# Router logits computed in token order, with the activations as the stationary operand

## The reference

```python
shared_out = _expert(x, shared_gate, shared_up, shared_down)
routing_probs = jax.nn.sigmoid(x @ router_w + routing_bias)   # (tokens, 3)
scores, indices = jax.lax.top_k(routing_probs, 2)
scores = scores / scores.sum(axis=-1, keepdims=True)
combine_w = (one_hot(indices, 3) * scores[..., None]).sum(axis=-2)
...                                # three routed experts, each silu(x@g)*(x@u)@d
combined = jnp.einsum('ebsh,bse->bsh', out_e, combine_w)
return shared_out + combined
```

## Time and profile before

| | us |
|---|---|
| median of three runs | 1599.58 (1598.1 to 1603.18) |
| profiled execution | 1602.77 |
| its span | 1601.0 |
| PE busy | 1579.0 (99%) |
| PE weight loads busy | 1483.5 (93%) |
| DVE busy | 1199.1 (75%) |
| ACT busy | 879.1 (55%) |
| POOL busy | 408.6 (26%) |
| PE clock granted, mean | 0.997 |

### The profile page before, as it was taken

One profiled execution on the slowest core, in us unless ns is written; L12 is line 12 of the kernel. 1 busy time (PEld: TensorE's weight loads), 2 busy tenths in 40 slices (PEclk: granted clock), 3 DMA queues, 4 the chain that ended last, 5 costly groups with the idle time before them and its releaser, 6 DMA issues.

```text
span 1601.0 us, 46493 instructions
## 1 busy us (share of the span) xinstructions
PE 1579.0 (99%) x16632; PEld 1483.5 (93%) x16632; DVE 1199.1 (75%) x3387; ACT 879.1 (55%) x1896; POOL 408.6 (26%) x647
## 2 busy tenths in 40 slices
PE   7999999999999999999999999999999999999999
PEld 7799999999999999999999999999999999998998
DVE  6777787777877777877777877777877777877765
ACT  4556555555555565555565555565555566555542
POOL 1232321223212323212323212323212323212320
PEclk9999999999999999999999999999999999999999
DMA  6311211112111111111111111111111111111000
GB/s 248 106 52 60 70 55 46 50 58 69 61 41 39 44 49 57 57 39 39 43 49 57 57 39 39 44 50 57 57 38 40 44 50 57 57 35 35 34 33 14
DMA packets 75382, 86.81 MB, mean 54 GB/s; under 512 B 12720, under 2 KB 64328, under 8 KB 75208
## 3 DMA queue, kind: packets, MB, share of 16 engines
q1 hardware_dynamic: 65192, 66.85, 12.2%
q10 hardware_dynamic: 10144, 19.34, 3.8%
HBM read 32.44 MB, written 12.51 MB: 28 GB/s over the span
## 4 chain that ended last, share of the span: by engine, by line
PE 91%; DMA 4%; DVE 3%; SPq 1%; issue 1%; ACT 0%; POOL 0%; DVEq 0%
PE ps L439 83%; PE ps L442 6%; DMA kt<-kt 3%; PE ps L646 2%; DVE kt L1233 1%; DMA h<-in_txt 1%; DVE o L1130 1%; SPq L373 0%; DVE rotated L1221 0%; DVE xt L1161 0%; DVE qk_split L1226 0%; DVE stats L1150 0%; DVE rotated L1193 0%; POOL rstd L1075 0%; DVE h L1254 0%
## 5 line engine op out<-in xcount | busy, mean ns | idle before, releaser
L439 PE MATMUL ps<-xt,wf 64*128 64x326 f32 x6912 | 595.9, 316 | 0.0
L439 PEld LDWEIGHTS ps<-xt,wf 64*128 64x128 f32 x6912 | 533.5, 186 | 10.9 <-ACT qt L840 5.5
L439 PE MATMUL ps<-w_down_s,ht 128*128 128x192 f32 (+1 forms) x2304 | 414.9, 329 | 0.0
L439 PEld LDWEIGHTS ps<-w_down_s,ht 128*128 128x128 f32 (+1 forms) x2304 | 350.9, 174 | 14.9 <-issue 0.2
L1107 DVE SCALAR_TENSOR_TENSOR gated<-tanh_g,ps 128x326 f32<-128x326 f32 x384 | 188.9, 492 | 132.7 <-ACT tanh_g L854 132.3
L865 ACT ACTIVATE probs<-ps 128x792 f32<-128x792 f32 (+1 forms) x384 | 254.5, 663 | 23.1 <-PE ps L439 23.1
L854 ACT ACTIVATE tanh_g<-ps 128x326 f32<-128x326 f32 x384 | 170.1, 443 | 169.0 <-PE ps L439 166.4
L1066 POOL TENSOR_TENSOR probs<-probs,causal 128x512 f32<-128x512 f32 x192 | 228.8, 1192 | 133.6 <-ACT probs L865 133.6
L847 ACT ACTIVATE rows<-h,rstd 128x192 f32<-128x192 f32 (+2 forms) x279 | 151.1, 564 | 194.7 <-POOL rstd L1077 192.3
L1060 POOL TENSOR_TENSOR probs<-probs,causal 69x140 f32<-69x140 f32 x192 | 89.1, 464 | 475.4 <-ACT probs L865 475.4
L1113 DVE TENSOR_TENSOR ht<-gated,ps 128x326 f32<-128x326 f32 x384 | 190.1, 495 | 13.1
(11 more groups left out here) (108 smaller groups left out, 2003.7 us busy)
## 6 DMA issues: line engine op xcount, KB each, us to landing
kt<-kt SPq DMA_DIRECT2D x384, 40.8 KB, 1.9
x_s<-in_xp ACTq DMA_DIRECT2D x36, 384.0 KB, 3.1
qt<-qt SPq DMA_DIRECT2D x130, 81.5 KB, 2.0
residual<-h SPq DMA_DIRECT2D x31, 288.0 KB, 2.4
out<-o SPq DMA_DIRECT2D x32, 192.0 KB
qt<-qt ACTq DMA_DIRECT2D x62, 81.5 KB, 2.0
kept_rows<-embed_rows SPq DMA_DIRECT2D x40, 96.0 KB, 1.7
h<-kept_rows SPq DMA_DIRECT2D x30, 95.2 KB
```

The lines of the kernel that those rows point to most:

```text
L439: return nc.tensor.matmul(dst, lhs, rhs, start=first, stop=last)
```

## The change

The router's operands trade places. For each of the three token tiles, six products take the tile's columns of `xt2` as the stationary operand and stream the 4 columns of `wr`: 18 products, whose results lie tokens on partitions. VectorE adds the bias (now a 128x4 tile, positive), 9 numbers per partition, into `route` (`route_logits`), at the end of its turn behind `keep_k`. ScalarE takes exp(-x) of these 9 numbers (`route_up`). `route_turn` with its three products, its bank, its signal and its two waits goes, and `route_sum` reads `route` in SBUF instead of PSUM, in place. Score piece 0 now waits for the bias addition instead of the exponential, and unit 2 takes over the wait for the third kt group from `route_turn`. A memset and a sign change of the opening go too.

```diff
+                for t in range(TILES):
+                    for j in range(BLOCKS):
+                        for x in range(2):
+                            last = mm(ps[0:TILE_COLS[t], ROUTER_BANK, t * R_COLS:(t + 1) * R_COLS],
+                                      xt2[:, j, x, tile_cols(t)], wr[:, j, :], j + x == 0, j + x == BLOCKS)
...
-            def route_turn(b, A):
-                pe.wait_ge(route_exp.sem, route_exp.at(b, 1))
-                if A:
-                    pe.wait_ge(kt_kept.sem, kt_kept.at(b + 1, GROUPS))
-                for t in range(TILES):
-                    last = mm(ps[:, ROUTE_BANK, t * P:t * P + R_COLS], route_e[0:H, t * P:(t + 1) * P], ident[0:H, 0:R_COLS],
-                              True, True)
...
+            def route_up(b):
+                act.wait_ge(route_seen.sem, route_seen.at(b, 1))
+                nc.scalar.activation(route[:, 1], route[:, 0], ACT.Exp, scale=-1.0).then_inc(route_exp.sem, 1)
...
+            def route_logits(b):
+                dve.wait_ge(router_done.sem, router_done.at(b, 1))
+                logits = shaped(ps[:], [[R_COLS, TILES], [1, EXPERTS]], ROUTER_BANK * 512)
+                v.tensor_tensor(route[:, 0], logits, shaped(router_bias[:], [[0, TILES], [1, EXPERTS]]),
+                                ALU.add).then_inc(route_seen.sem, 1)
...
-                dve.wait_ge(route_turned.sem, route_turned.at(b, 1))
-                e = shaped(ps[:], [[P, TILES], [1, EXPERTS]], ROUTE_BANK * 512)
-                v.tensor_scalar(route[:, 1], e, 1.0, None, ALU.add).then_inc(route_seen.sem, 1)
+                dve.wait_ge(route_exp.sem, route_exp.at(b, 1))
+                v.tensor_scalar(route[:, 1], route[:, 1], 1.0, None, ALU.add).then_inc(route_raised.sem, 1)
...
@@ turn of VectorE, behind keep_k(2, b1, KEEP_BANK)
+                    route_logits(b2)
```

More of the change, by code:

```diff
@@ L70 @@
 KEEP_BANK = [6, 7, 2, 3, 6, 7]
-XT_BANK, YT_BANK, EMBED_BANK, ROUTER_BANK, ROUTE_BANK, PROJ_BANK = 6, 4, 2, 0, 7, 0
+XT_BANK, YT_BANK, EMBED_BANK, ROUTER_BANK, PROJ_BANK = 6, 4, 2, 0, 0
 SPLIT_PARTS = len(SPLIT_AT) - 1
@@ L111, in build @@
         bias_rows = sb("bias_rows", [P, 2, DIM])
-        router_bias = sb("router_bias", [R_COLS, 1])
+        router_bias = sb("router_bias", [P, R_COLS])
         cos_t = sb("cos_t", [P, TILES, HEAD_DIM // 2])
@@ L211, in build @@
         router_done = signal("router_done", 1)
-        route_turned = signal("route_turned", 1)
         n1_applied = signal("n1_applied", 1)
@@ L249, in build @@
         route_seen = signal("route_seen", 1)
+        route_raised = signal("route_raised", 1)
         gate_used = signal("gate_used", UNITS)
@@ L508, in unit @@
                         pe.wait_ge(qt_kept.sem, qt_kept.at(b + 1, GROUPS))
-                    pe.wait_ge(route_seen.sem, route_seen.at(b, 1))
+                        pe.wait_ge(kt_kept.sem, kt_kept.at(b + 1, GROUPS))
                 else:
@@ L524, in score @@
                 elif F:
-                    pe.wait_ge(route_exp.sem, route_exp.at(b - 1, 1))
+                    pe.wait_ge(route_seen.sem, route_seen.at(b - 1, 1))
                 if n % 2 == 0:
@@ L699, in turn @@
                         unit(k, b3, at, D, A)
-                        if k == 0:
-                            route_turn(b3, A)
                     if A:
@@ L935, in turn @@
                 if A:
-                    act.wait_ge(router_done.sem, router_done.at(b2, 1))
-                    nc.scalar.activation(route_e[0:R_COLS, 0:COLS], ps[0:R_COLS, ROUTER_BANK, 0:COLS], ACT.Exp, scale=-1.0,
-                                         bias=router_bias[:, 0:1]).then_inc(route_exp.sem, 1)
+                    route_up(b2)
             def start_norm1(b):
@@ L1047, in _ @@
                 keep_high(j, xt2[:, j, 0, :], N2_BANK[j], n2_turned, 0, xt2_hi)
[L1048 to L1051, removed]
+            route_up(0)
             turns(act, turn)
@@ L1373, in turn @@
                     sum_up(6, b3, L)
+                    if A:
+                        route_logits(b2)
             def split_ffn(j):
@@ L1393, in _ @@
             v.memset(row_sum[:], 1.0)
-            v.memset(route_e[:], 0.0)
             dve.wait_ge(s_bias, 16)
@@ L1406, in _ @@
             dve.wait_ge(s_const, 16 * 6)
-            v.tensor_scalar(router_bias[:], router_bias[:], -1.0, None, ALU.mult)
             v.tensor_copy(ident_r[:], ident[:]).then_inc(s_halve, 1)
@@ L1462, in _ @@
             v.tensor_scalar(w_down_s[:], w_down_s[:], 0.5, None, ALU.mult).then_inc(s_halve, 1)
+            route_logits(0)
             turns(dve, turn)
@@ L1518 @@
         "w_route": w_route, "w_down": w_down,
-        "b_router": b_router.reshape(R_COLS, 1),
+        "b_router": np.tile(b_router, (P, 1)),
         "rot_cos": rot_cos, "rot_sin": rot_sin, "mask": mask,
```

8 lines of the change are left out of this document (1 added, 7 removed).

## The result

| | before | after |
|---|---|---|
| median of the runs, us | 1601.28 (4 runs, 1598.10 to 1603.18) | 1618.46 (4 runs, 1617.06 to 1624.39) |
| profiled execution, us | 1602.77 | 1624.39 |
| its span, us | 1601.0 | 1622.6 |
| PE clock granted, mean | 0.997 | 0.985 |

The changed kernel is slower: ratio 1.0105, 95% interval 1.0087 to 1.0124. I had predicted 1601.8, between 1596.5 and 1619.5, with "within 0.3%" as the likeliest case. The time lies in the range, at the number of rival 1 (1618.5), but the likeliest case did not happen, and rival 1's mechanism is only a small part of the loss, as will be seen. The prediction also named a wait on VectorE ahead of units 4 to 6 as a sign of being wrong; there are two such waits, 0.8 us in all.

The account below looks back on a forecast made before the run. TensorE, busy 99% of the span, was taken as the bound. Router +0.80 less route_turn 0.66 gave +0.14 us in 12 turns, less elsewhere: about +2.2 on 1599.6, so 1601.8 us, range 1596.5 to 1619.5.

Parts of the forecast that it names:

- within 0.3%: Whole kernel: a time within 4.8 us of before, not to be told from no change; chance of same 0.45.
- rival 1: VectorE's last small routing operation (L1283) stands behind GpSimd's large mask; unit 6 at 10.3, about +19 us, 1618.5; chance 0.27.
- a wait on VectorE ahead of units 4 to 6: Sign in TensorE's waits: a wait on DVE ahead of these units would make the prediction wrong.
- The router, 1.80 us and +0.80: TensorE, first router product to unit 0: 18 products paced by stationary loads take 1.80 us instead of 1.00.
- upper bound of 0.95: Router's added time per turn if all 18 loads go at 0.12 us without a discount.
- route_turn, 0.66 us: TensorE between unit 0 and score piece 0: without its six loads, unit 1 and everything behind come 0.66 earlier.
- The DMA of kt: Score piece 0 waits for the DMA in 19 of 31 turns; up to 0.14 us of that wait vanishes.
- VectorE ahead of unit 6: VectorE gets back 0.6 us from mask collisions; up(3) ends at 9.15, ahead of unit 6 at 9.27.
- the walk: VectorE's new turn: route_sum 3.08 to 3.40, last small operation at 4.25, large mask 4.20 to 5.39.
- The margin of 0.05 us: VectorE's L1283 at 4.25 against GpSimd's large mask at 4.20; the times rest on sums of ten terms.
- What costs nothing: VectorE at the turn's end: the last expert's sums still end near 1.33, ahead of unit 1 at about 1.6.

Follow-up runs that it names:

- second kernel: Changed kernel with router operand padded to 128 columns, plus the last expert's sums moved ahead of route_logits: 1632.38 us, 1.0174 of before.
- third: As the second kernel, with the routing chain moved from units 0 and 1 to units 6 to 10: 1602.60 us, 0.9988 of before.
- fifth kernel: As the second kernel, with route_sum alone moved ahead of VectorE's products of unit 0: 1604.04 us, 0.9999 of before.
- sixth kernel: As the third, with the router's moving operand narrow again, 4 columns instead of 128: 1617.90 us, 1.0091 of before.
- first kernel: Changed kernel with the router's moving operand padded with zeros from 4 to 128 columns: 1612.13 us, 1.0047 of before.
- fourth kernel: Kernel before the change, with 18 narrow products added behind its own router, results unused: 1659.66 us, 1.034 of before.

## Why the prediction was right or wrong

**The router, 1.80 us and +0.80:** right (1.78). The rate of loading by the earlier trace rows carried over to a place with other streams. The upper bound of 0.95 was summed wrongly: all 18 loads at 0.12 give 2.16, with the 0.10 until unit 0 that is 1.26 more than before; 0.95 needs the six loads of 70 columns to stay near 0.06.

**route_turn, 0.66 us:** right where nothing else held unit 1: the last product of unit 1 starts at 2.92 behind unit 0 in turns 0, 1 and 30 and at 2.93 in the second, third and fifth kernels, 3.60 before.

**The DMA of kt:** right in kind, too small in size. TensorE's wait for it fell from 3.5 us in 9 waits to 1.4 in 2; behind 440 us, in the looped turns, from 2.6 in 8 to none (its weight loads alone still show 1.7 in 7, of 3.8 in 11). Rows of the waits, before and after:

```profile
PE ps L439 <- DMA kt<-kt: 3.5, 9, 0.9
```

```profile
PE ps L438 <- DMA kt<-kt: 1.4, 2, 1.2
```

The prediction let at most 0.14 us of each wait vanish, and counted nothing for the turns with a longer one. In the sixth kernel, which has the same narrow router and neither late sums nor a collision, the last product of unit 1 starts at 2.92 to 3.20 in the turns at full clock; before it was 3.60 to 4.25. So of the up to 0.65 that this wait had added, 0.28 at most was left, and turns that had waited long became shorter.

**VectorE ahead of unit 6:** the walk held to some hundredths: route_sum from 3.08 to 3.40, L1277 at 4.25. The margin of 0.05 us was the right place to doubt, and its answer is plain: started behind the mask by 0.05 to 0.07 us (second kernel, turns 0, 1 and 30 here), the operation stands to the mask's end; 0.16 ahead of it (turn at 631.36) or 0.09 (turn 28), it passes. The first kernel has the closest case: in its turn 7 both start at 431.46, the operation 0.003 us ahead, and it passes in 0.16. The walk's own mask at 4.20 would have lost; I should have read L1277 at 4.25 against 4.20 as a collision, since in every row the one that started first kept the way, and given rival 1 the greater chance. Rival 1's own sum has a slip too: up(1) at 6.4 against unit 4 at 6.17 is a wait of 0.23 there and not 0.37, which is the difference at unit 6 (10.3 against 9.93). The Trainium skill (SBUF — State Buffer, "Who interferes with whom") says that the order of issue decides who blocks. The runs agree in both directions: the operation takes 0.15 us when it starts ahead of the mask and 1.16 when it starts behind.

**"What costs nothing" failed.** The prediction had the last expert's sums end near 1.33 as before and unit 1 unharmed. They end at 1.76, since VectorE now comes to the loop's branch only behind route_logits, which waits for the router, and is then idle; the trace has the idle time in VectorE's waits:

```profile
DVE o L1118 <- issue: 11.0, 26, 0.5
```

That is 0.42 us, 26 times; it makes unit 1 late by 0.2 (shown by the second kernel, where the sums stand ahead and unit 1 is on time). Before, the same branch stood ahead of the sums with no idle time, so it takes both, the branch and the wait ahead of it; this is read off the rows and no run separates the two. By luck the late unit 1 moved the masks out of L1277's way: the looped turns came out neutral (+0.08 us on average in the 16 turns with full clock, +0.07 predicted), for a reason that I hadn't. The average is luck too: single turns differ from before by -0.33 (turn 8) to +0.43 (turn 24), where the prediction had 0 to +0.14.

**The cause that no step and no rival named** is the clock: +15.6 of the 19.5 us in the profiled turns, 16.5 us by the sixth kernel against the third, about 9 by the first against the changed kernel. The last two numbers differ in part because the first kernel also got two further turns with the collision (+1.6 us) and longer padded turns (16 of them by 0.09, +1.4); with these added back it is about 12. The rest fits the clocks of the runs, 0.986 to 0.987 in the sixth kernel and 0.988 to 0.989 in three of the changed kernel's four. The prediction took TensorE's time from durations at full clock on the strength of a mean of 0.997 before, and did not ask whether the new instructions would keep it. The rival's number was met by another mechanism, so a time close to 1618.5 was no proof of it; only the stretches by clock and the sixth kernel told the two apart.

What stays open is why only some turns have the stretch. The routers ahead of turns 2 to 7 end the turns 1 to 6, which embed two tiles and not one and are 1.5 us longer; whether these have it each time because of when they come or of what stands ahead of the router in them isn't known. In the changed kernel and in the sixth it was nearly the same turns.

## What to carry to other kernels

When an edit swaps a product's operands so that it streams few columns, look up the granted clock stretch by stretch and not only the busy share: here such a run of products cost 1.5 us behind it in ten turns, and padding the moving operand to 64 columns took this away at no cost that these runs show. Where one engine's instruction keeps another's standing and the one that starts first wins, write both start times side by side and don't build on a margin under 0.1 us; moving one small instruction (the fifth kernel) gave 28 us. And an instruction that waits is better not put ahead of a loop's branch on its engine if work behind the branch is due.

## What the runs showed of the hardware

- The granted clock fell to half for 3.4 us at a time (6.8 in the fourth kernel) behind 18 products of 4 columns, with TensorE 100% busy before and in it. In the profiled executions this followed the router in ten of 32 turns with 4 columns (after, the sixth), in two with 32, in one (the last) with 64, and in none with 128.
- A TENSOR_SCALAR of 9 fp32 elements from SBUF to SBUF takes 0.16 to 0.17 us alone and 0.32 when it starts under a GpSimd mask, until the mask's end; a TENSOR_TENSOR of 3 elements 0.15 alone, 1.16 with the large mask. A start 0.05 us behind the mask's is enough.
- VectorE was idle for 0.42 us at its loop's branch when the instruction ahead of the branch had waited for TensorE (26 turns); before, with no such wait ahead of it, there was no idle time at the same branch.
- Three products on 128 rows between products on 64 rows took as long as six on 64 rows (0.66 us).
